# Rows of minus the maximum: turned by TensorE and placed by two DMAs, with the matmuls for the maximum first in each step

## The reference

```python
# sublayer 1 (plain attention)
scores = jnp.einsum('bhqd,bhkd->bhqk', q, k) / np.sqrt(HEAD_DIM)
attn = jax.nn.softmax(scores, axis=-1)
# sublayer 2 (the same with a causal mask, then a mixture of experts)
scores = jnp.where(causal, scores, -jnp.inf)
# sublayer 6: eight attention experts, each token's output is the sum over its top 2
q = (x @ qw.T + qb_).reshape(B, S, H, Dh).transpose(0, 2, 1, 3)
scores = jnp.einsum('bhqd,bhkd->bhqk', q, k) * scale
p = jax.nn.softmax(scores, axis=-1)
o = jnp.einsum('bhqk,bhkd->bhqd', p, v)
o = o.transpose(0, 2, 1, 3).reshape(B, S, E) @ ow.T + ob_
return (acc + o * g[..., None], None)
```

## Time and profile before

| | |
|---|---|
| time, median of 3 runs | 5381.61 us (5370.77 to 5388.61) |
| profiled execution | 5380.44 us, of which the span from first to last instruction is 5378.8 |
| mean granted TensorE clock | 0.795 of full |
| busy: PE, PEld | 3682.4 us (68%), 1989.6 us |
| busy: DVE, ACT, POOL | 3231.9 us (60%), 2557.0 us (48%), 698.0 us (13%) |
| DMA: packets, of which under 512 B | 188780, 109592 |
| DMAs that place rows of minus the maximum | 1160 in C, 1032 in A and B |

### The profile page before, as it was taken

How to read it: one execution, slowest core, us unless ns; L and a number is a source line. 1 busy time by engine, 2 the same in 40 slices (tenths; PEclk the granted TensorE clock), 3 DMA queues, 4 the chain that set the end, 5 groups by cost and what they waited for, 6 DMA issues and landing times. The chain is left out here.

```text
span 5378.8 us, 143641 instructions
## 1 busy us (share of the span) xinstructions
PE 3682.4 (68%) x55035; PEld 1989.6 (37%) x55035; DVE 3231.9 (60%) x3991; ACT 2557.0 (48%) x4624; POOL 698.0 (13%) x1502
## 2 busy tenths in 40 slices
PE   1688888417997965558441677777777777777747
PEld 0344444203455732224331333333333334333314
DVE  2677777516892149974321666666666666666644
ACT  1567776304774432112110455656565656566532
POOL 0000000001100007740200010111111111111120
PEclk6788888757998977778675787878888888788767
DMA  3000000110000012200333433333433343433320
GB/s 54 12 8 6 7 8 6 23 35 10 11 6 13 20 53 107 94 4 4 61 105 108 87 82 80 81 79 82 86 79 80 82 86 75 84 82 80 79 53 20
DMA packets 188780, 286.62 MB, mean 53 GB/s; under 512 B 109592, under 2 KB 154334, under 8 KB 163930
## 3 DMA queue, kind: packets, MB, share of 16 engines
q1 hardware_dynamic: 183466, 272.07, 22.2%
q0 software_dynamic: 4656, 5.18, 0.4%
HBM read 220.57 MB, written 41.52 MB: 49 GB/s over the span
## 5 line engine op out<-in xcount | busy, mean ns | idle before, releaser
L801 ACT ACTIVATE channels_qk<-psum 128x512 f32<-128x512 f32 (+1 forms) x3908 | 2107.7, 591 | 1304.7 <-PE psum L683 1158.1
L858 DVE TENSOR_REDUCE l2f_chunk_max<-psum 128x2 f32<-128x1024 f32 x1168 | 1387.5, 1220 | 765.8 <-PE psum L656 762.1
L858 DVE TENSOR_REDUCE chunk_max<-psum 128x2 f32<-128x1024 f32 (+2 forms) x848 | 951.4, 1159 | 306.5 <-PE psum L656 236.8
L683 PE MATMUL psum<-l2f_q_parts,l2f_k_parts 51*128 51x128 bf16 x9224 | 530.9, 242 | 484.5 <-DMA l2f_q_parts<-l2f_minus_max_rows 343.0
L704 PE MATMUL psum<-channels_qk,l2f_v_and_ones 128*9 128x128 f32 x18448 | 839.4, 309 | 30.8 <-issue 30.8
L683 PEld LDWEIGHTS psum<-l2f_q_parts,l2f_k_parts 51*128 51x128 bf16 x9224 | 298.2, 103 | 873.8 <-issue 536.7
L704 PEld LDWEIGHTS psum<-channels_qk,l2f_v_and_ones 128*9 128x9 f32 x18448 | 425.9, 97 | 402.9 <-issue 209.6
L656 PE MATMUL psum<-l2f_k_parts,l2f_q_parts 48*128 48x512 bf16 x2336 | 527.3, 447 | 20.1 <-DMA l2f_q_parts<-l2f_gathered_q_parts 12.1
L704 PE MATMUL psum<-channels_qk,v_and_ones 128*9 128x128 f32 x12560 | 533.5, 293 | 0.1
L656 PE MATMUL psum<-k_parts,q_parts 48*128 48x512 bf16 (+3 forms) x1696 | 345.2, 406 | 241.8 <-DMA q_parts<-q_parts_dram 225.9
L683 PE MATMUL psum<-q_parts,k_parts 51*128 51x128 bf16 x6280 | 339.7, 231 | 221.1 <-DMA q_parts<-minus_max_rows 166.4
(11 more groups left out here) (474 smaller groups left out, 3466.5 us busy)
## 6 DMA issues: line engine op xcount, KB each, us to landing
l2f_k_parts<-l2f_k_parts_dram SPq DMA_DIRECT2D x298, 192.0 KB
l2f_v_and_ones<-expert_v_dram SPq DMA_DIRECT2D x37, 1152.0 KB, 5.2
l2f_k_parts<-l2f_k_parts_dram SPq DMA_DIRECT2D x298, 128.0 KB
l2f_k_parts<-l2f_k_parts_dram SPq DMA_DIRECT2D x298, 64.0 KB
l2f_q_parts<-l2f_minus_max_rows SPq DMA_DIRECT2D x1160, 0.4 KB
q_parts<-minus_max_rows SPq DMA_DIRECT2D x1032, 0.4 KB
l1a_bc_rows<-ssm_rows_dram SPq DMA_DIRECT2D x16, 1024.0 KB, 5.6
expert_v_dram<-l2f_v_and_ones SPq DMA_DIRECT2D x8, 1152.0 KB, 6.9
```

Source lines behind the costliest of these rows:

```text
L683: last = nc.tensor.matmul(c.ps[:, bank[j], (2 * kk + pp) * P:(2 * kk + pp + 1) * P], kx(k)[64 * j:64 * j + ROWS + 3, pair, kt * P:(kt + 1) ...
L801: nc.scalar.activation(at.prob[:, s % 4, j, 0:kts, :].rearrange("p k q -> p (k q)"), c.ps[:, ring.bank(i, n), 0:kts * 2 * P], ACT.Exp, sca ...
L858: v.tensor_reduce(at.mx[:, 4 * g + 2 * pp:4 * g + 2 * pp + 2, chunk], c.ps[:, 2 * (n % 2):2 * (n % 2) + 2, 0:span.width(tile, chunk)], X, ...
```

## The change

The rows are turned by TensorE, not by VectorE. `minus_max_parts` is laid out as 12 columns for each group, and one transpose writes them as [12, 128] to a ring bank; ScalarE copies it to `minus_max_rows`, now [12, 4, 128], and two DMAs (one for each half of the heads) place the rows of a group. The turn is a new extra of the ring, `rows0` to `rows3`, due at step 2 of each group (or the group's last step, where it has fewer). In A and C it is for the same group as before (g + 1); in B it comes one group later than before (rows of group g + 2, `late` = 2). SyncE waits for ScalarE's copy on `s2_read`. Before the loop the first groups are turned in banks 4 to 6 with semaphores of their own. Second, TensorE's order in a step becomes: first pass, `second_pass(s + 1)`, extras, `weighted_values(s - 1)`; only the second pass of the next tile's first step comes after the extras.

```diff
-        self.mparts = sb(ctx, "minus_max_parts", [P, 4, 32], BF16)
-        self.mrow = sb(ctx, "minus_max_rows", [P, 4, 32], BF16)
+        self.mparts = sb(ctx, "minus_max_parts", [P, 4, 2, 3, 2], BF16)
+        self.mrow = sb(ctx, "minus_max_rows", [12, 4, P], BF16)
...
+    def rows_in(self, g):
+        ahead, group = divmod(g + self.lead - self.late, 4)
+        return group, ahead
     def due(self, i, s):
+        steps = self.span.steps(i)
+        g, u = s // steps, s % steps
+        names = []
+        if u == min(2, steps - 1):
+            group, ahead = self.rows_in(g)
+            if not self.span.causal or i + ahead < NT:
+                names.append(f"rows{group}")
...
-    ML = 16 * 8
+    ML = 16 * 2
...
-            def load_max(g, tile, k):
-                slot = slot_of(tile, k)
-                sp.wait_ge(mrow_ready, tile * G + (g + 1))
+            def load_max(g, slot):
                 for j in range(2):
-                    for b in range(4):
-                        sp.dma_start(at.q[64 * j + ROWS:64 * j + ROWS + 3, slot, 2 * g:2 * g + 2, 32 * b:32 * b + 32],
-                                     at.mrow[32 * b + 6 * j:32 * b + 6 * j + 6, g, :]).then_inc(max_loaded[g], 16)
+                    sp.dma_start(at.q[64 * j + ROWS:64 * j + ROWS + 3, slot, 2 * g:2 * g + 2, :],
+                                 at.mrow[6 * j:6 * j + 6, g, :]).then_inc(max_loaded[g], 16)
+            def load_later_max(i, g, k):
+                group, tile, parity = rows_of(i, g, k)
+                if exists(tile):
+                    sp.wait_ge(s2_read, ring.read_when(i, ring.place(i, f"rows{group}")))
+                    load_max(group, slot_of(tile, parity))
...
+            def turn_rows(g, bank):
+                return nc.tensor.transpose(c.ps[:, bank, :].bitcast(BF16)[0:12, 0:P],
+                                           at.mparts[:, g, :, :, :].rearrange("p j n a -> p (j n a)"), c.identb[:, :])
...
+                elif name[:4] == "rows":
+                    pe.wait_ge(mparts_ready, count)
+                    turn_rows(int(name[4]), bank).then_inc(s2_ready, 1)
...
                 for s in range(G * steps):
-                    if s < last_step:
-                        second_pass(s + 1, i, k)
-                    elif exists(i + 1):
-                        second_pass(0, i + 1, 1 - k)
...
                     group, tile, parity, load_round = first_pass_of(i, g, k, r)
                     if exists(tile):
                         for unit in share(2 * span.chunks(tile), u, steps):
                             first_pass(group, unit, tile, parity, load_round)
+                    if s < last_step:
+                        second_pass(s + 1, i, k)
+                    for name in ring.due(i, s):
...
+                    if s == last_step and exists(i + 1):
+                        second_pass(0, i + 1, 1 - k)
...
+                elif name[:4] == "rows":
+                    nc.scalar.activation(at.mrow[:, int(name[4]), :], bank.bitcast(BF16)[0:12, 0:P], ACT.Copy).then_inc(s2_read, 1)
...
-            def turn_max(g, tile):
-                dve.wait_ge(mparts_ready, tile * G + (g + 1))
-                v.transpose(at.mrow[:, g, :], at.mparts[:, g, :]).then_inc(mrow_ready, 1)
```

More of the change, by code:

```diff
@@ L221 @@
 class AttentionConstants:
-    FILLS = 4
+    FILLS = 3
     def __init__(self, c, at, buffers):
@@ L233, in gpsimd @@
         g.memset(at.v[:, :, :, :, :], 1.0).then_inc(self.filled, 1)
-        g.memset(at.mparts[:, :, :], 0.0).then_inc(self.filled, 1)
         g.memset(at.one[:, :], 1.0).then_inc(self.filled, 1)
@@ L323, with __init__ @@
     BANK0, BANKS = 4, 3
-    def __init__(self, span, routed):
-        self.span = span
+    def __init__(self, span, lead, routed):
+        self.span, self.lead, self.late = span, lead, 2 if span.causal else 1
         self.extras = {4: "out", 13: "outT", 17: "proj", 21: "q"} if routed else {4: "out"}
@@ L333, in __init__ @@
             self.size = len(self.fills(0))
+            assert self.size % self.BANKS == 0
+    def rows_in(self, g):
+        ahead, group = divmod(g + self.lead - self.late, 4)
+        return group, ahead
     def due(self, i, s):
+        steps = self.span.steps(i)
[5 more added lines that the diff above has]
+                names.append(f"rows{group}")
         if not self.span.causal:
-            return self.extras.get(s)
-        return "out" if i > 0 and s == min(4, 4 * self.span.steps(i) - 2) else None
+            return names + ([self.extras[s]] if s in self.extras else [])
+        return names + (["out"] if i > 0 and s == min(4, 4 * steps - 2) else [])
     def fills(self, i):
@@ L349, in fills @@
                 order += [(s + 1, 0), (s + 1, 1)]
-            if self.due(i, s):
-                order.append(self.due(i, s))
+            order += self.due(i, s)
         return order
@@ L366, in free_when @@
     def free_when(self, i, n):
[L368 to L371, removed]
+        return self.number(i, n + 1)
     def read_when(self, i, n):
@@ L398, in attention_loop @@
     span = Span(tri is not None)
-    ring = Ring(span, routed is not None)
+    ring = Ring(span, lead, routed is not None)
     SLOTS = 2 if tri is None else 3
@@ L406, in first_pass_of, with rows_of @@
         return (group, i + 1, 1 - k, r + k) if ahead else (group, i, k, r)
-    def max_before(i, g, k):
-        ahead, group = divmod(g + lead - 1, G)
+    def rows_of(i, g, k):
+        group, ahead = ring.rows_in(g)
         return (group, i + 1, 1 - k) if ahead else (group, i, k)
@@ L453, in attention_loop @@
     s2_ready, s2_read, pv_done = c.sem("attn_s2_ready"), c.sem("attn_s2_read"), c.sem("attn_pv_done")
-    negm_ready, mparts_ready, mrow_ready = c.sem("attn_negm_ready"), c.sem("attn_mparts_ready"), c.sem("attn_mrow_ready")
+    negm_ready, mparts_ready = c.sem("attn_negm_ready"), c.sem("attn_mparts_ready")
+    first_rows_turned, first_rows_copied = c.sem("attn_first_rows_turned"), c.sem("attn_first_rows_copied")
     oT_copied, oT_filled = c.sem("attn_oT_copied"), c.sem("attn_oT_filled")
@@ L504, in tile_loads @@
                 for g in range(G):
-                    group, tile, parity = max_before(i, g, k)
-                    if exists(tile):
-                        load_max(group, tile, parity)
+                    load_later_max(i, g, k)
                     if g == 0:
@@ L516, in routed_loads @@
                 for g in range(G):
-                    load_max(*max_before(i, g, k))
+                    load_later_max(i, g, k)
                     if g == 0:
@@ L544, in _ @@
                 load_q(1, 1)
-            for g in range(lead - 1):
-                load_max(g, 0, 0)
+            for g in range(lead - ring.late):
+                sp.wait_ge(first_rows_copied, g + 1)
+                load_max(g, 0)
             rounds = each_tile(sp, routed_loads if routed else tile_loads)
@@ L596, in split_max @@
                 pool.wait_ge(negm_ready, tile * G + (g + 1))
-                parts = at.mparts[:, g, 0:12].rearrange("p (j n a) -> p n j a", j=2, n=3)
-                split(at.negm[:, 4 * g:4 * g + 4].rearrange("p (a j) -> p j a", j=2), [parts[:, n] for n in range(3)],
+                split(at.negm[:, 4 * g:4 * g + 4].rearrange("p (a j) -> p j a", j=2), [at.mparts[:, g, :, n, :] for n in range(3)],
                       at.rest[:, g, :].rearrange("p (j a) -> p j a", j=2), link, mparts_ready)
@@ L755, in whole_tile @@
                             first_pass(group, unit, tile, parity, load_round)
+                    if s < last_step:
+                        second_pass(s + 1, i, k)
+                    for name in ring.due(i, s):
+                        if name == "proj":
+                            fill(name, i, ring.place(i, name), k, ring.read_when(i, ring.place(i, "outT")))
+                        elif name[:4] == "rows":
+                            rows, tile, _ = rows_of(i, g, k)
+                            fill(name, i, ring.place(i, name), k, tile * G + (rows + 1))
+                        else:
+                            fill(name, i, ring.place(i, name), k, r * 16 + 32)
+                    if s == last_step and exists(i + 1):
+                        second_pass(0, i + 1, 1 - k)
                     if s == 0 and (tri is None or i > 0):
@@ L775, in _ @@
                     first_pass(g, unit, 0, 0, 0)
+                if g > 0 and g - 1 < lead - ring.late:
+                    pe.wait_ge(mparts_ready, g)
+                    turn_rows(g - 1, ring.BANK0 + 3 - g).then_inc(first_rows_turned, 1)
+            pe.wait_ge(first_rows_copied, lead - ring.late)
             if routed:
@@ L838, in _ @@
                     nc.scalar.activation(routed.qT[:, :], c.ps[:, ring.BANK0 + k, 0:P], ACT.Copy).then_inc(first_q_copied, 1)
+            for g in range(lead - ring.late):
+                act.wait_ge(first_rows_turned, g + 1)
```

(5 more changed lines are left out.)

## The result

The changed kernel takes 4928.6 us (median of 4 runs, 4905.5 to 4942.6) against 5383.0 (4 runs): ratio 0.915, 95% interval 0.911 to 0.920. It is faster by 8.5%. 4765 was forecast, with 4690 to 4850 as the forecast's own band: the time lies outside that band, inside the stated range of 4650 to 4950, and inside the band of the rival "a wait takes the place" (4880 to 5040). The profiled execution took 4940.6 us with a span of 4939.0, 440 less than before.

The account below looks back on a forecast made before the run. TensorE's second pass was taken to wait for rows that SyncE issues late, with a low clock afterwards. From 5380.4 us, loops A, C and B save 139, 443 and 33, giving 4765 us; range 4650 to 4950.

Parts of the forecast that it names:

- a wait takes the place: Loop C: SyncE's queries and keys delay group 1's rows by 2.5 us in every tile; 4880 to 5040 us; chance 0.20.
- wrong if rows of group 1 still come late in each tile of C: Loop C: one of three signs that would refute the prediction; its sum put a 0.6 us wait in every second tile.
- under 60 us of waits for rows: Loop C: total wait of TensorE's second passes for rows would fall below 60 us, from 343.
- The bound and SyncE's issues: Second passes wait for rows SyncE issues late; two DMAs at 0.74 us make a group cost 1.5 us, not 5.9.
- The chain in A: Loop A: parts ready 0.3 us before the turn at worst, rows landing 1.2 us early, so every wait for rows goes.
- An extra's price in TensorE: TensorE's ring: each rows' transpose costs 0.35 us, between nothing and 0.86; four in a tile make 1.4 us.
- The order costed at nothing: TensorE's step: first pass ahead of second adds no instruction and gives nothing where there is no wait; costed at nothing.
- The rows of the next group are issued until 19.4 and land at 20.6: Loop C, group 1: rows wanted at 20.5, so 0.1 us late; 0.6 wait and 1.6 of slow steps every second tile.
- The jump: Loop C's jump back, once in two tiles: 6.2 us stop and five slow steps (3.9), halved to 5.05 a tile.
- the rival of a clock kept low by short ring waits: Loops A and C: short ring waits keep the clock low, C keeping 191 us and A 56: 5010 us; chance 0.07.
- Loop B: First tiles go from 5.9 to 4.5 us a group; 34 plus some 8, less 9 for extras: 33 us gained.
- More gain: Extras cost nothing (- 73 in A and C), or C's jump is as short as A's (54): 4650 to 4690; chance 0.09.

Follow-up runs that it names:

- small keys of group 1: Changed kernel, but in loop C only the key loads issued just ahead of group 1's rows move 256 of 2048 tokens: 4803.7 us, ratio 0.891.
- Small keys: Changed kernel, but all key DMAs inside loop C move 256 of 2048 tokens each, with the same number of issues: 4709.2 us, ratio 0.875.

## Why the prediction came out as it did

The direction, the bound and loop A came out as argued. Loop C did not: by the prediction's own sign ("wrong if rows of group 1 still come late in each tile of C") it failed there, and the signs "under 60 us of waits for rows" (109) and "clock above 0.9 in both loops" (0.89 in C) failed with it. That 4928.6 lies in the stated range is in part luck: a term put at nothing, the order, gave back 108 us. With the old order the time is 5036, outside the range.

*The bound and SyncE's issues: right.* Two a group, 0.74 us each in C (L494, median 0.738; 0.695 before) though each carries four times the data. *The chain in A: right.* Parts were there at 628.58, the turn at 629.92, 1.3 us early; from 172 to 850 us TensorE has no wait for rows, and the turn can be a step later for nothing.

*An extra's price in TensorE: 0.35 counted, 0.49 measured.* First passes of A around a turn:

```profile
629.09 0.39 PE L666 MATMUL psum<-k_parts,q_parts 48*128 48x512 bf16 x2
...
630.51 0.39 PE L666 MATMUL psum<-k_parts,q_parts 48*128 48x512 bf16 x2
...
631.90 0.39 PE L666 MATMUL psum<-k_parts,q_parts 48*128 48x512 bf16 x2
```

The step with the turn takes 1.42 us, the next 1.39, where ScalarE's copy stands before a bank, against 1.16: 0.26 + 0.23. Four in a tile are 2.0, not 1.4, and account for nearly all of A's 43.2 against 42.5.

*The order costed at nothing: wrong.* It is worth 108 us here and 118 alone. I had argued that with no wait it gives nothing, which A bears out, and then applied this to C, in which I myself left waits for rows and the jump. I had written that a second pass that must wait no longer holds back VectorE, and put no number on it.

*"The rows of the next group are issued until 19.4 and land at 20.6": the step that failed in C.* I had costed SyncE's issues and taken 1.2 us for landing from a place where the keys in front had been issued 6 us earlier; the old eight issues had been spacing the rows from the keys. When the last of them was issued, from 3616 to 3618, the key bytes were through, as the DMA share (the last but one number) shows:

```profile
3616.00:3618.00 2.00, 0.00 (x0) 0.00 (x0) 0.00 (x0) 0.00 (x0) 0.00 (x0) 0.70 0.03 5
```

With two issues the rows are on the keys' heels: 5.3 us. I had named the keys just ahead in the queue as what may hold the rows up, and sized it far too small: I had a wait of 0.6 in every second tile, 0.3 a tile; it is 109 / 36 = 3.0. The rival "a wait takes the place" was right about the place (group 1 of nearly every tile, and group 0 of every second) and about the size (109 / 52 = 2.1 us, and it had said 2.5); it gave SyncE's issues as reason, and it was the bytes: with the same issues and small keys of group 1, 18 us of waits are left.

*The jump: counted too low, and not by the change.* The sum kept one stop of 6.2 us and five slow steps. The kernel before already lost 8.5 us a jump for "issue" and this one loses 8.8, so a tile has (8.8 - 6.2) / 2 = 1.3 more than in the sum. Together with the rows that is 4.0 of the 5.0 missed; that the rest is low clock is an estimate, by what is left over. Key bytes were under way at the jump in the kernel before as well:

```profile
3588.00:3590.00 2.00, 0.00 (x0) 0.00 (x0) 0.00 (x0) 0.00 (x0) 0.00 (x0) 0.50 0.76 140
```

So they are a cost that the change left. Small keys remove both effects, and C takes 46.0 us; the sum without late rows is 46.8, with a jump of 3.6 in it some 45.5.

That the stops for "issue" are code being fetched is inferred, not shown. For it: they shrink with key bytes, recur at the same steps of the loop's body, and the profile lists two queues of instructions on the DMA engines (8.00 and 1.38 MB). Not explained by bytes alone: ScalarE's second stop lasts until 3550.44, while from 3548 to 3550 the DMA engines are 4% busy.

*The clock* came back where waits went (A) and didn't fall by itself: the rival of a clock kept low by short ring waits is out, as A holds four more ring extras a tile at 0.94, and at 1.00 throughout from 624 to 662 us, where there is no jump. By the rule on cycling through PSUM banks in the Trainium skill, "TensorE: Matmul & The Clock Gate", section "A second HAM failure mode: psum-queue depth-cycling", it should have gone up and down between groups of matmuls; this trace disagrees.

*Loop B: 33 forecast, 47 measured.* The 15 intervals give 28, and the first tile 19 more. Its first second passes that want rows start at 1042.07, 1046.15 and 1050.30, 4.1 us apart, where I had 4.5; 10 waits of up to 1.9 us for rows stay.

*A slip in a rival.* "More gain" was given 4650 to 4690, but with the short jump alone (- 54) it is 4711. Nothing hung on it.

## What to carry to other kernels

When a queue of small DMAs is the bound, count issues first: here a row DMA cost some 0.7 us with 32 queries and with 128, and merging eight into two paid for a longer way through two engines. Then ask what stood between a bulk load and the small transfer behind it: issues that are removed were also a gap. And in an in-order engine, put work that feeds others ahead of the instruction that may wait; in A, where there is no wait, it cost nothing (43.2 us a tile with either order).

## What was not expected of the hardware

Bulk loads slowed an engine that uses no data of theirs: ScalarE's stops for "issue" in C fell from 182 to 61 us (35 stops each time) when key bytes fell to an eighth, be it all of them or only those near the jump.
